# Records kept in token order and gathered by the experts, in place of records scattered into the experts' slots

## The reference

```python
def xattn(query, ctx):                      # 16 heads of 8
    q, k, v = heads(query @ Wq + bq), heads(ctx @ Wk + bk), heads(ctx @ Wv + bv)
    attn = softmax(einsum('bhnd,bhsd->bhns', q, k) * 8 ** -0.5)
    return merge(einsum('bhns,bhsd->bhnd', attn, v)) @ W_out + b_out

def ffn(x):                                 # tokens in order of (batch, position)
    logits = tokens @ Wg
    gates = softmax(logits)
    idx = argmax(gates, axis=1)
    mask1 = one_hot(idx, 8)
    locations1 = cumsum(mask1, axis=0) - 1.0          # a token's place in its expert
    mask1 = mask1 * (locations1 < 512)                # later tokens get nothing
    ...
    expert_in = einsum('tec,th->ech', dispatch, tokens)
    hidden = relu(einsum('ech,ehf->ecf', expert_in, W1) + b1)
    expert_out = einsum('ecf,efh->ech', hidden, W2) + b2
    return einsum('tec,ech->th', combine, expert_out) # combine = gate * dispatch

x = x + tanh(g_xattn) * xattn(layernorm(x), ctx)
x = x + tanh(g_ffn) * ffn(layernorm(x))
```

## Time and profile before

| | us |
|---|---|
| median of 3 runs | 315.67 |
| lowest, highest | 314.27, 316.78 |
| the profiled execution: its own time | 313.11 |
| its span, first to last instruction | 311.3 |

### The profile page before, as it was taken

One profiled execution on the slowest core, in us unless ns is written; L12 is line 12 of the kernel. 1 busy time (PEld: TensorE's weight loads), 2 busy tenths in 40 slices (PEclk: granted clock), 3 DMA queues, 4 the chain that ended last, 5 costly groups with the idle time before them and its releaser, 6 DMA issues. The chain is left out here.

```text
span 311.3 us, 8092 instructions
## 1 busy us (share of the span) xinstructions
PE 245.3 (79%) x2864; PEld 157.6 (51%) x2864; DVE 208.0 (67%) x718; ACT 150.1 (48%) x347; POOL 181.8 (58%) x235
## 2 busy tenths in 40 slices
PE   1748989699999779879879798896106999999940
PEld 0425736446647546546546455553003577777730
DVE  4676668579999799799779969963300455555610
ACT  4452776477776766766765545572001422222100
POOL 6626928409839949949949907447750055555671
PEclk9998579899999999999999959996555999999985
DMA  4653846924726506616405511147216255554310
GB/s 114 176 153 99 238 144 204 277 72 107 221 56 188 163 31 167 181 35 185 135 29 154 158 34 41 55 133 170 73 47 168 69 169 172 165 169 126 98 51 15
DMA packets 50919, 39.25 MB, mean 126 GB/s; under 512 B 9698, under 2 KB 47223, under 8 KB 50880
## 3 DMA queue, kind: packets, MB, share of 16 engines
q1 hardware_dynamic: 47168, 28.67, 33.8%
q0 software_dynamic: 3712, 10.07, 9.9%
HBM read 13.72 MB, written 12.65 MB: 85 GB/s over the span
## 5 line engine op out<-in xcount | busy, mean ns | idle before, releaser
L645 ACT ACTIVATE prob<-TS 128x512 f32<-128x512 f32 x128 | 72.1, 590 | 49.5 <-PE TS L480 47.8
L759 DVE TENSOR_REDUCE negm<-S 128x4 f32<-128x512 f32 x128 | 82.0, 683 | 15.6 <-PE S L465 13.9
L496 PE MATMUL O<-prob,vals 128*32 128x128 f32 x1024 | 56.2, 295 | 3.7 <-ACT oraw L654 3.6
L1154 POOL DMA_INDIRECT out_dram<-fin,tok x32 | 31.6, 988 | 11.5 <-issue 9.9
L1081 POOL DMA_INDIRECT rec_dram<-rec,slot x32 | 32.3, 1009 | 10.1 <-issue 6.4
L496 PEld LDWEIGHTS O<-prob,vals 128*32 128x32 f32 x1024 | 21.3, 111 | 26.4 <-issue 10.9
L260 POOL TENSOR_TENSOR rest_k<-full_k,parts_k 128x512 f32<-128x512 f32 x7 | 8.0, 1147 | 45.2 <-ACT parts_k L628 45.2
L465 PE MATMUL S<-kp,qp 62*128 62x128 bf16 x512 | 31.8, 231 | 1.3 <-DVE negm L759 1.0
L480 PE MATMUL TS<-qp,kp 64*128 64x128 bf16 x512 | 29.2, 227 | 3.3 <-DMA qp<-mrow 3.2
L593 PE MATMUL X<-w2s,qp 128*128 128x128 f32 x256 | 29.7, 275 | 0.0
L593 PEld LDWEIGHTS X<-w2s,qp 128*128 128x128 f32 x256 | 29.2, 192 | 0.5 <-issue 0.5
(11 more groups left out here) (134 smaller groups left out, 485.8 us busy)
## 6 DMA issues: line engine op xcount, KB each, us to landing
kp<-parts_k SPq DMA_DIRECT2D x48, 128.0 KB, 2.5
qp<-parts_q SPq DMA_DIRECT2D x48, 128.0 KB, 2.6
rec_dram<-zeros POOLq DMA_DIRECT2D x8, 516.0 KB, 5.5
xr<-rec_dram SPq DMA_DIRECT2D x8, 260.0 KB, 3.7
x_sb<-in_x_dram SPq DMA_DIRECT2D x8, 256.0 KB, 4.0
c_sb<-in_ctx_dram SPq DMA_DIRECT2D x8, 256.0 KB, 3.9
out_dram<-rec SPq DMA_DIRECT2D x8, 256.0 KB, 2.7
w1s<-in_L_ffn_W_dram SPq DMA_DIRECT2D x8, 256.0 KB, 3.9
```

The lines of the kernel that those rows point to most:

```text
L496: mm = nc.tensor.matmul(o_out[i * HV:(i + 1) * HV, u * L:(u + 1) * L], vals[G % 2][:, k, h, :], prob[n % 2][:, h * L:(h + 1) * L], start=( ...
L645: nc.scalar.activation(prob[n % 2][:, first:first + 4 * L], TS[:, a, :], ACT.Exp).then_inc(a_exp, 1)
L759: V.tensor_reduce(negm[n % 2][:, first:first + 4], S[:, a, :].rearrange("p (h k) -> p h k", k=L), AX.X, ALU.max, negate=True).then_inc(v_r ...
L1154: G_.indirect_dma_start(out_rows, bass.IndirectOffsetOnAxis(tok[p][:, t:t + 1], 0), fin[p][:, t, :], None, bounds_check=T - 1, oob_is_err= ...
```

## The change

Records are stored in token order, and it is the experts that look up which token holds each slot.

- `rec_dram` gets one plain store per group, issued by SP at j = 3 after waits for `g_xn2` and `v_gate`. The zero fill and the scatters go. A record has 264 columns and no token code.
- `place` makes, for each token, the row (place modulo 128) and the column (expert x 4 + tile) of its slot, both as one-hot matrices: `one_r`, 128 x 4 x 128 bf16, and `one_c`, 128 x 4 x 32; `coded` is `one_c` times the batch number + 1, and `one_c` times the token's number in the batch. A new task `idx` (j = 3, bank 1) multiplies `one_r` with `coded` on PE, four matmuls a group, so each slot gets its token's number; `held` on DVE (next j = 0) adds it to `holder`. At the end `tokens_of_slots` turns it into `from_row` and `to_row`.
- `xe`, `xr` and SP's loads of them go. POOL's `rows_in(e)` fetches four tiles of 128 records with indirect DMAs into `gx`, with four buffers: experts 0 to 3 ahead, the others after the `rows_out` of expert e - 4. For expert 0 each tile has a semaphore of its own, and PE turns it when it is there.
- `norm2` calls `scaled` right after the power, before the two wide passes, and not at j = 1; `place` waits for the exponentials only at its end.
- PE does four matmuls of 128 x 512 with `w1s[0]`, whose result nobody reads, before turn(0).
- The constants are loaded in two DMAs; the first holds only the identity.

```diff
-REC = 2 * P + 2
+REC = 2 * P + 8
...
-        rec_v = rec_dram.rearrange("(e t p) c -> e p t c", t=ET, p=P)
+        rec_v = rec_dram.rearrange("(n p) c -> p n c", p=P)
...
-            third = {0: ("xl", g), 1: ("pos", g - 2)}.get(j)
+            third = {0: ("xl", g), 1: ("pos", g - 2), 3: ("idx", g - 2)}.get(j)
...
-            sp.dma_start(cst[:], consts).then_inc(s_cst, 16)
+            sp.dma_start(cst[:, 0:P], consts[:, 0:P]).then_inc(s_cst, 16)
...
+                sp.dma_start(cst[:, P:], consts[:, P:]).then_inc(s_more, 16)
...
+                if j == 3 and is_group(g - 2):
+                    sp.wait_ge(g_xn2, g - 1)
+                    sp.wait_ge(v_gate, g - 1)
+                    sp.dma_start(rec_v[:, bass.ds((g - 2) * GB, GB), :], rec[(g - 2) % 3][:]).then_inc(rec_out[(g - 2) % 3], 16)
...
+                elif name == "idx":
+                    pe.wait_ge(v_one, idx + 1)
+                    pe.wait_ge(v_coded, idx + 1)
+                    for k in range(GB):
+                        mm = nc.tensor.matmul(X[:, 1, 0:2 * COLS], one_r[:, k, :], coded[:, k, :, :].rearrange("p i c -> p (i c)"),
+                                              start=(k == 0), stop=(k == GB - 1))
+                    mm.then_inc(p_idx, 1)
...
+            pe.wait_ge(w1_in[0], 16)
+            pe.wait_ge(v_red, 4 * B)
+            for _ in range(4):
+                nc.tensor.matmul(S[:, 1, :], ident, w1s[0][:], start=True, stop=True)
             turn(0)
...
             def place(G):
...
+                spread = [P, GB, COLS]
                 dve.wait_ge(v_pos, G + 1)
+                V.tensor_reduce(loc[:], at_e[:], AX.X, ALU.add).then_inc(v_place, 1)
+                done(1)
+                V.tensor_tensor(passed[:], loc[:].unsqueeze(2).broadcast_to(spread), steps, ALU.is_ge).then_inc(v_place, 1)
+                done(2)
+                V.tensor_reduce(tile[:], passed[:], AX.X, ALU.add).then_inc(v_place, 1)
+                done(3)
+                V.scalar_tensor_tensor(row[:], tile[:], -float(P), loc[:], ALU.mult, ALU.add).then_inc(v_row, 1)
+                V.scalar_tensor_tensor(col[:], choice[:], float(ET), tile[:], ALU.mult, ALU.add).then_inc(v_place, 1)
+                done(4)
+                V.tensor_tensor(one_c[:], iota_c, col[:].unsqueeze(2).broadcast_to(spread), ALU.is_equal).then_inc(v_place, 1)
+                done(5)
...
+                V.tensor_tensor(coded[:, :, 0, :], one_c[:], iota_p[:, G * GB + 1:G * GB + GB + 1].unsqueeze(2).broadcast_to(spread),
+                                ALU.mult)
+                V.tensor_scalar(coded[:, :, 1, :], one_c[:], own, None, ALU.mult).then_inc(v_coded, 1)
+                dve.wait_ge(v_row, G + 1)
+                V.tensor_tensor(one_r[:], iota_p.unsqueeze(1).broadcast_to([P, GB, P]),
+                                row[:].unsqueeze(2).broadcast_to([P, GB, P]), ALU.is_equal).then_inc(v_one, 1)
                 dve.wait_ge(a_lexp, G + 1)
-                V.tensor_reduce(loc[:], at_e[:], AX.X, ALU.add)
                 V.tensor_reduce(lsum[:], lexp[:], AX.X, ALU.add).then_inc(v_place, 1)
-                V.tensor_copy(rec[G % 3][:, :, 2 * D + 1], token_code[:, bass.ds(G * GB, GB)])
...
+            def held(G):
+                dve.wait_ge(p_idx, G + 1)
...
+                V.tensor_tensor(holder[:], X[:, 1, 0:2 * COLS], holder[:], ALU.add).then_inc(v_idx, 1)
...
                 root(G, mv2, rs2, v_mv2, g_e2).then_inc(g_rs2, 1)
+                scaled(G)
...
-                for i in ((c - 1,) if 0 <= c - 1 < ZEROED else ()):
-                    zero_records(i)
-                if j == 1 and is_group(g - 2):
-                    scaled(g - 2)
...
+            def rows_in(e):
+                if e >= 4:
+                    pool.wait_ge(v_res, e - 3)
+                    pool.wait_ge(p_eT, e - 3)
+                for t in range(ET):
+                    G_.indirect_dma_start(gx[e % 4][:, t, :], None, rec_dram,
+                                          bass.IndirectOffsetOnAxis(from_row[:, e * ET + t:e * ET + t + 1], 0),
+                                          bounds_check=T - 1, oob_is_err=False).then_inc(first_in[t] if e == 0 else gx_in[e % 4], 16)
...
+            for p in range(3):
+                pool.wait_ge(rec_out[p], 16 * len(range(p, NG, 3)))
+            pool.wait_ge(v_from, 1)
+            fence()
+            for e in range(4):
+                rows_in(e)
...
             for e in range(E):
                 for h in range(2):
                     rows_out(e, h)
+                if e + 4 < E:
+                    rows_in(e + 4)
```

More of the change, by code:

```diff
@@ L149, in flamingo_kernel @@
         loc = sb("loc", [P, GB])
-        over = sb("over", [P, GB])
-        base = sb("base", [P, GB])
-        slot = [sb(f"slot{i}", [P, GB], U32) for i in range(3)]
+        passed = sb("passed", [P, GB, COLS])
+        tile = sb("tile", [P, GB])
+        col = sb("col", [P, GB])
+        row = sb("row", [P, GB])
+        one_c = sb("one_c", [P, GB, COLS])
+        one_r = sb("one_r", [P, GB, P], BF16)
+        coded = sb("coded", [P, GB, 2, COLS], BF16)
+        holder = sb("holder", [P, 2 * COLS])
+        found = sb("found", [P, COLS])
+        nobody = sb("nobody", [P, COLS])
+        from_row = sb("from_row", [P, COLS], U32)
+        to_row = sb("to_row", [P, COLS], U32)
         w1s = [sb(f"w1s{i}", [P, F]) for i in range(2)]
@@ L175, in flamingo_kernel @@
         x1_out = [sem(f"x1_out{i}") for i in range(3)]
-        sent = [sem(f"sent{i}") for i in range(3)]
+        rec_out = [sem(f"rec_out{i}") for i in range(3)]
+        first_in = [sem(f"first_in{i}") for i in range(ET)]
+        gx_in = [sem(f"gx_in{i}") for i in range(4)]
+        v_row, v_one, v_coded, p_idx, v_idx = sem("v_row"), sem("v_one"), sem("v_coded"), sem("p_idx"), sem("v_idx")
+        v_gate, v_found, v_from, v_to = sem("v_gate"), sem("v_found"), sem("v_from"), sem("v_to")
         p_cT, p_xT, p_q, p_k, p_v = sem("p_cT"), sem("p_xT"), sem("p_q"), sem("p_k"), sem("p_v")
@@ L506, in step @@
                         2: [t for t in groups if t[0] in ("xT", "q", "xl") or t[0] == "k" and j == 2],
-                        3: [t for t in groups if t[0] == "pos"]}
+                        3: [t for t in groups if t[0] in ("pos", "idx")]}
                 if is_batch(c):
@@ L565, in turn @@
             def turn(e):
[L567 removed]
+                if e >= 1:
+                    rows_arrived(pe, e)
                 if e >= 2:
@@ L882, in place @@
-                done(1)
-                V.tensor_scalar(over[:], loc[:], float(CAP), float(NONE), ALU.is_ge, ALU.mult)
-                V.scalar_tensor_tensor(base[:], choice[:], float(CAP), loc[:], ALU.mult, ALU.add).then_inc(v_place, 1)
-                V.reciprocal(rec[G % 3][:, :, 2 * D], lsum[:])
-                done(2)
-                V.tensor_tensor(slot[G % 3][:], base[:], over[:], ALU.add).then_inc(v_slot, 1)
+                done(6)
+                V.reciprocal(rec[G % 3][:, :, 2 * D], lsum[:]).then_inc(v_gate, 1)
@@ L903, in step @@
                     positions(g - 2)
+                if j == 0 and is_group(g - 3):
+                    held(g - 3)
                 if is_batch(c):
@@ L968, in _ @@
                     V.tensor_copy(bout_g[:, D:DE], O[:, 0, E:2 * E]).then_inc(v_wl, 1)
+            held(NG - 1)
+            tokens_of_slots()
             def relus(e):
@@ L1025, in _ @@
             G_ = nc.gpsimd
-            def fence():
-                return G_.tensor_tensor(fence_p[:], pool_c[:, 0, 0:1], pool_c[:, 0, 0:1], ALU.add).then_inc(g_fence, 1)
             def root(H, mv, rs, ready, e):
@@ L1068, in norm2 @@
                 G_.tensor_tensor(to, to, rs2[:, 1, :].unsqueeze(2).broadcast_to(spread), ALU.mult).then_inc(g_xn2, 1)
-            def scatter(G, k):
-                p = G % 3
-                if k == 0:
-                    if G == 0:
-                        for q in range(3):
-                            pool.wait_ge(sent[q], zeros_sent(q))
-                    pool.wait_ge(g_xn2, G + 1)
-                    pool.wait_ge(v_slot, G + 1)
-                    if G == NG - 1:
-                        pool.wait_ge(g_fence, NG - 1)
-                    fence()
-                G_.indirect_dma_start(rec_dram, bass.IndirectOffsetOnAxis(slot[p][:, k:k + 1], 0), rec[p][:, k, 0:REC], None,
-                                      bounds_check=T - 1, oob_is_err=False).then_inc(sent[p], 16)
             def step(c):
```

128 lines of the change are left out of this document (59 added, 69 removed).

## The result

| | before | after |
|---|---|---|
| median, us | 316.23 (314.27 to 320.43, 4 runs) | 323.28 (322.26 to 326.66, 4 runs) |
| the profiled execution: time, span | 313.11, 311.3 | 323.64, 320.7 |
| last POOL issue | 304.15 | 314.22 |

The ratio is 1.0263, with an interval of 1.0156 to 1.0369: the change costs 7 us. The forecast was 326, in a range of 317 to 333. The spans differ by 9.4 us; the forecast's sum was 10.9. Medians in this document are over all executions, while ratios and their intervals leave out executions over 1.5% above the fastest of the same kernel, in most of which the granted clock was lower too.

A forecast was written before the change was run, and what follows sets the result against it. PE bounds the expert stage, with POOL hidden, and DVE is tightest in attention. POOL becoming the expert stage's bound adds 10.1 us, attention 0.8: +10.9 on the median 315.67 gives 326 us, range 317 to 333.

The forecast's parts named there:

- the main case: Whole kernel: slower, 326 us, with POOL's indirect DMAs bounding the expert stage; chance 55%.
- POOL is the bound: Expert stage, experts 0 to 3: POOL needs 10.4 us each for fence, four scatters and four gathers, against PE's 7.45.
- I take 1.28: Expert stage: gathers on POOL follow each other every 1.28 us, like the scatters; bounds 1.0 and 1.4.
- rivals A: Expert stage: gathers cheaper to issue, 1.0 us apart, and PE then the bound: 319.5 us; chance 10%.
- C: Expert stage: a gather costs POOL far less than a scatter, PE sets the pace, not slower: 314.5 us; chance 8%.
- t0: Start of the first gather in the expert stage, forecast at 230.8 us; the last issue follows 83.5 us later.
- The last group: End of attention: POOL's wide passes hold `passed` until 222.7, row and col until 224.0; the store then takes 4.0 us.
- the three stalled ones about 0: Attention groups: in three groups DVE's added 2.15 us and the removed copy and logits stalls of 2.3 about cancel.
- Rival B: Landings of 4 us, and two-input DVE instructions meeting POOL's wide passes in every group: 332 us; chance 15%.
- Rival D: Attention stage: removing the zero fill gives 7 us and DVE's additions are half absorbed: 321 us; chance 12%.
- The extra matmuls: Before the first tile: four matmuls run under 8 us at half clock on idle PE, ending about when it comes; counted 0.
- POOL does not notice: Start of expert stage: hidden(0) ending about 2 us earlier would not matter, as POOL's 16 gathers last until 251.

The follow-up runs named there:

- a0: The changed kernel again, no edit, in the first set of runs: 332.75 us, ratio 1.0549 to the kernel before.
- a1: The changed kernel again, no edit, in the second set of runs: 324.13 us, ratio 1.0251 to the kernel before.
- a2: The changed kernel again, no edit, in the third set of runs: 330.44 us, ratio 1.0455 to the kernel before.
- e1: The changed kernel without the 16 gathers of experts 4 to 7, which reuse the rows of experts 0 to 3: 312.2 us, ratio 0.9925.
- e6: The kernel before with scaled logits issued ahead of the wide passes and the token code copied by ScalarE: 304.16 us, ratio 0.9607.
- e3: The changed kernel with the eight zero fills put back on POOL, into a tensor nobody reads: 341.49 us.
- e2: The changed kernel without the four extra matmuls ahead of turn(0): 333.1 us, ratio 1.0614 to the kernel before.
- e8b: The changed kernel with three unused matmuls ahead of each turn of experts 4 to 7, run in the third set: 332.57 us.
- e9: The changed kernel with the scaled logits issued a step later again, behind POOL's two wide passes: 333.86 us, ratio 1.0531.

## Why the prediction was right, and where it was off

The verdict (slower), the main case and the place were right. The sum, term by term, on the spans of the two profiles of the result:

| term | forecast | measured |
|---|---|---|
| front (zero fill) | -4.5 | -4.7 |
| seven groups (DVE's additions less the stalls) | +5.3 | +0.2 |
| comparison of the last group to first gather | 10.8 | 11.5 |
| first gather to last issue | 83.5 | 87.2 |
| last issue to the end | as before, 7.2 | 6.5 |

The differences are -0.2 - 5.1 + 0.7 + 3.7 - 0.7 = -1.6, and 10.9 - 1.6 is the 9.4 of the spans, within rounding. So two terms were off by 5.1 and 3.7 us and largely cancelled: that the total came within 2 us of the sum is luck. So is a part of the small differences: the front varied by 4.3 us between profiles of the same code, and the third term was 9.9 in a0, a1 and a2. In two of the four sets the time was 330 to 333, at the upper edge of the range, for a reason that the prediction didn't have (below).

**POOL is the bound** held, and e1 shows it by undoing it. The step "I take 1.28" measured 1.30: the size of a row doesn't count (1019 ns busy for the gathers of 1056 B, 998 for scatters of 512 B), and rivals A (1.0 apart) and C (a gather nearly free) fall with it. The 3.7 us come from three places. The first scatter stands at t0 + 22.8 in place of 20.9: POOL's fence waited 1.08 us for expert 0's results, which PE's first hidden layer, at half clock, had made late, and the 16 gathers and the fence took 0.4 us more each than in the sum. From there to the last gather POOL needed 41.0 us in place of 39.9, mostly from 10.6 us an expert where the sum had 10.4. And the end, from the last gather (290.87) to the last issue, took 23.35 us in place of 22.7, in small pieces: 3.13 for 2.9 until the rows were there, 7.67 for 7.45 until PE's outputs of expert 6 began, and 2.52 for 2.4 until the fence. I had taken PE's early surplus as cover for its clock without asking what the first scatter waits for.

**The last group** went as forecast, instruction by instruction: one pass stalls `passed`, the next stalls `row` and `col`, and both ended where said. The store was the difference (4.5 in place of 4.0).

**The groups** were mis-sized. The step "the three stalled ones about 0" set the additions against two stalls worth 2.3 us a group. Those three shrank by 1.2, 1.1 and 0.9 us, while the fifth grew by 0.6 where I had +0.8 (the first grew 1.6, the sixth 1.6, the seventh shrank by 0.5 where I had +0.5). So 3.1 of the 5.1 us lie in the three stalled groups. With these stalls gone and nothing added (e6) they take 21.1; with the additions 22.3. So the rest of the change costs 1.0 to 1.5 us in each of these groups (2.15 counted), and 145.7 - 136.0 = 9.7 us in all seven. The stalls were worth 9.5 over the seven, more than the 2.3 in three groups that I saw: in e6 the last two groups are shorter as well (18.4 to 17.7, 13.7 to 11.6). Rival B (332, collisions in every group) didn't come; the long executions reach its time from another place. The bounds of this part were added up wrongly, too: 0 to +9 for the groups and -9 to -1.5 for the front make -9 to +7.5, not -7 to +8.

**The zero fill** gave 4.7 in the two profiles of the result, as forecast, but that is one draw: with the spread of the front it is 3 to 9 us, 5.5 between the means, and e3 puts the fills at 6 to 10. Rival D's 7 us isn't excluded. I would not carry any of these numbers.

**The extra matmuls** were counted at 0, and e2 agrees within its noise. The step behind it failed in its timing: they were to run at half clock for under 8 us and to end about when the first tile comes. They ran 5.97 us, brought the clock to full on the way and ended 2.74 us before the first tile, and in that wait the clock fell again. "POOL does not notice" failed as well: POOL's fence waited 1.08 us for the results behind this hidden layer.

Not forecast: the two lengths of the expert stage, 87 and 96 to 98 us. The runs show that in the long one PE's results come late at expert 2 and again from expert 3 on, that it happened in two sets of runs of four, in every kernel of these sets that gathers 32 tiles (a0, e2, e3, a2, e8b, e9), that in e1, with 16 gathers, only the first of the two delays came, and that filling PE's gaps doesn't prevent it. What slows PE there stays open. The second and third sets are recorded under the same chip number and gave one kind each, so the chip alone isn't shown to decide. Either way the kernel is slower: at best by 7 to 8 us, at worst by 17.

## What to carry to other kernels

Before moving work to an engine with a low busy share, take what one instruction costs there from start to start, and hold the sum against the bound of that stage: POOL's share of the span fell from 58% to 54%, and it became the bound of the expert stage. In this kernel a 4-column instruction of DVE beside a wide pass of POOL took up to 1.95 us and held up all that follows it in order; the two small edits that were aimed at such waits gave 4% alone (e6). When a kernel's time differs between sets of runs, let it run beside each experiment: with a0 alone, the long stage would have passed for an effect of PE's gaps.

## What the runs showed of the hardware that I had not expected

- PE's records can stand at full speed while its results are late. In a2 the records of expert 3's hidden layer are 0.86 us a bank, and the relus that wait for them 3.50 us apart where 1.72 was due. What waits for PE tells its pace better than PE's own rows.
- A granted clock regained by matmuls was lost in the next wait: four of 128 x 512 over 5.97 us brought it from 0.50 to 1.00, and after 2.74 us of idle PE it was 0.50 again. The hidden layer behind it took 2.08 for two matmuls, in place of 1.02.
- PE's waits of 2.22 and 2.38 us for rows, in the changed kernel of the result, and of 2.12 in a1 were followed by outputs of 5.36 to 5.37 us for 32 matmuls, a large part of them at a granted clock of 0.50; behind waits of 0.79 and 1.52 us they took 3.74, and behind the filled gaps of e8 as good as that.
- An indirect DMA of 128 rows took 1.0 us of POOL, and 1.28 to 1.30 from one to the next, for rows of 512 B and of 1056 B alike; the first gather took 1.26, and the first scatter, behind a wait of POOL, 1.15.
